# Two graph attention layers: the edge bytes are turned by VectorE in 32x32 blocks, masked on ScalarE, in groups of eight row tiles

## The reference

```python
def _L0_gnn_ref(input, W, a, adj, M):        # input: h, 8192 x 128; M = 8192
    h = input @ W
    e = jax.nn.leaky_relu((h[:M] @ a[:OUT, 0])[:, None] + (h @ a[OUT:, 0])[None, :], negative_slope=ALPHA)
    valid = (adj[:M] > 0) & (h.sum(axis=1) != 0)[None, :]
    att = jnp.where(valid, jax.nn.softmax(jnp.where(valid, e, NEG), axis=1), 0.0)
    L = valid.sum(axis=1).astype(h.dtype)
    top = att.max(axis=1)
    attention = jnp.where(att >= THR, att, 0.0) * L[:, None]
    attention = jnp.where((top > THR)[:, None], attention, 0.0)
    return jax.nn.elu(h[:M] + attention @ h)

def _L1_gnn_ref(h, adj, W, a):
    Wh = h @ W
    e = jax.nn.leaky_relu((Wh @ a[:F_out, 0])[:, None] + (Wh @ a[F_out:, 0])[None, :], negative_slope=ALPHA)
    return jax.nn.softmax(jnp.where(adj > 0, e, NEG_INF), axis=1) @ Wh

h = jnp.maximum(_layernorm(x, axis=-1), 0.0)     # x: 8192 x 128 f32, adj: 8192 x 8192 int32
x = x + _L0_gnn_ref(h, L0_gnn_W, L0_gnn_a, adj, 8192)
h = jnp.maximum(_layernorm(x, axis=-1), 0.0)
x = x + _L1_gnn_ref(h, adj, L1_gnn_W, L1_gnn_a)
```

## Time and profile before

| | us |
|---|---|
| median of 3 runs (2136.21 to 2138.7) | 2136.89 |
| the profiled execution, its own time | 2139.07 |
| its span, first to last instruction | 2137.3 |
| TensorE busy | 2010.9 (94%) |
| VectorE busy | 1561.5 (73%) |
| ScalarE busy | 806.9 (38%) |
| GpSimd busy | 638.6 (30%) |

### The profile page before, as it was taken

One profiled execution on the slowest core, in us unless ns is written; L12 is line 12 of the kernel. 1 busy time (PEld: TensorE's weight loads), 2 busy tenths in 40 slices (PEclk: granted clock), 3 DMA queues, 4 the chain that ended last, 5 costly groups with the idle time before them and its releaser, 6 DMA issues. The chain is left out here.

```text
span 2137.3 us, 43514 instructions
## 1 busy us (share of the span) xinstructions
PE 2010.9 (94%) x17812; PEld 2003.4 (94%) x17812; DVE 1561.5 (73%) x2452; ACT 806.9 (38%) x950; POOL 638.6 (30%) x263
## 2 busy tenths in 40 slices
PE   5699999999999999999965699999999999999997
PEld 4699999999999999999965699999999999999997
DVE  6687777777777777777747677777777777777775
ACT  4677777777777777777734000000000000000000
POOL 0675655575655575656510000000000000000000
PEclk9899999999999999999987799999999999999998
DMA  7889888899888899888832522323222323222230
GB/s 227 331 341 375 318 329 318 334 373 362 334 316 327 323 384 359 323 328 327 331 130 79 190 69 70 99 80 100 80 81 60 98 79 99 80 73 79 68 99 11
DMA packets 112206, 447.75 MB, mean 209 GB/s; under 512 B 8320, under 2 KB 57984, under 8 KB 62592
## 3 DMA queue, kind: packets, MB, share of 16 engines
q1 hardware_dynamic: 112000, 444.89, 56.4%
HBM read 365.04 MB, written 79.82 MB: 208 GB/s over the span
## 5 line engine op out<-in xcount | busy, mean ns | idle before, releaser
L984 PE MATMUL psum<-h_all,arena 128*128 128x129 f32 x8192 | 960.0, 275 | 0.2 <-DVE arena L1007 0.2
L1163 PE MATMUL psum<-h_all,arena 128*128 128x129 f32 x8192 | 919.4, 275 | 24.7 <-DVE arena L1180 24.7
L1163 PEld LDWEIGHTS psum<-h_all,arena 128*128 128x128 f32 x8192 | 917.9, 192 | 26.4 <-issue 17.3
L984 PEld LDWEIGHTS psum<-h_all,arena 128*128 128x128 f32 x8192 | 937.5, 192 | 1.2 <-issue 0.5
L1007 DVE SCALAR_TENSOR_TENSOR arena<-arena,rho_col,psum 128x512 f32<-128x512 uint8 (+1 forms) x1024 | 693.8, 742 | 235.6 <-PE psum L970 218.3
L1180 DVE SCALAR_TENSOR_TENSOR arena<-arena,rho_col 128x1024 f32<-128x1024 f32 (+1 forms) x512 | 653.3, 1284 | 235.4 <-PE psum L1163 222.9
L911 POOL TENSOR_SCALAR arena<-arena 128x2048 uint8<-128x2048 int32 x256 | 637.6, 2526 | 441.8 <-DMA arena<-in_adj_dram 293.4
L929 ACT ACTIVATE arena<-arena 128x2048 bf16<-128x2048 uint8 x256 | 487.8, 1906 | 35.1 <-POOL arena L911 35.1
L940 ACT ACTIVATE arena<-psum 128x1024 uint16<-128x1024 uint16 x256 | 261.1, 1020 | 251.0 <-DVE arena L1007 250.4
L970 PE MATMUL psum<-ident,arena 128*128 128x128 f32 x1024 | 154.4, 274 | 14.5 <-POOL arena L911 14.5
L970 PEld LDWEIGHTS psum<-ident,arena 128*128 128x128 f32 x1024 | 121.1, 142 | 14.7 <-POOL arena L911 14.7
(11 more groups left out here) (100 smaller groups left out, 191.8 us busy)
## 6 DMA issues: line engine op xcount, KB each, us to landing
arena<-in_adj_dram SPq DMA_DIRECT2D x256, 1024.0 KB, 9.8
edgesT<-arena SPq DMA_DIRECT2D x64, 1024.0 KB, 7.6
arena<-edgesT SPq DMA_DIRECT2D x64, 1024.0 KB, 8.8
arena<-r_mid SPq DMA_DIRECT2D x2, 3072.0 KB, 13.8
h_mid<-h_all SPq DMA_DIRECT2D x16, 256.0 KB, 2.3
arena<-in_x_dram SPq DMA_DIRECT2D x16, 256.0 KB, 3.1
arena<-h_mid SPq DMA_DIRECT2D x16, 256.0 KB, 3.9
x_mid<-arena SPq DMA_DIRECT2D x16, 256.0 KB, 2.4
```

What stands on the lines that cost most here:

```text
L984: last = nc.tensor.matmul(acc_tile(g, G0, k), wTs[m % WRING][:, k * P:(k + 1) * P], h_all[:, j, :], start=(j == 0 and k % 2 == 0), stop=(j ...
L1163: last = nc.tensor.matmul(acc_tile(g, G1, k), wTs[m % RING][:, k * P:(k + 1) * P], h_all[:, j, :], start=(j == 0 and k % 2 == 0), stop=(j ...
```

## The change

**Layout.** The partitions of a piece are no longer 128 rows of one row tile. A row tile is now 32 rows out of each quarter of the matrix (row `a*2048 + t*32 + i` with a in 0..3), and a piece of adjacency has, on its 128 partitions, four blocks of columns by 32 rows, 1024 columns each (0.5 MB, in 4 KB rows). With the words laid out so, turning every 32 x 32 block in place of the 128 x 128 one gives the same bytes at the place where a form wants them. x, h and the outputs are read or written by quarters of 32 partitions where they must follow.

**Masks.** ScalarE writes the bytes itself, as sigmoid(200 a - 100), straight out of the int32 piece, and counts with the same instruction's accumulator (`mask_piece`). GpSimd has no part in layer 0 any more. The counts are then in four parts on the wrong partitions: VectorE adds the halves and four small products on TensorE with a constant matrix `rows_of` bring them together (`join_counts`).

**Turns.** VectorE turns 1024 words per instruction (`turn_edges`), eight instructions for each *chunk* (eight row tiles by half of the columns, 32 pieces), two halves of four row tiles each; they go between the forms at fixed tiles (`turn_at`). The result lies in SBUF in five slots `edges` and is stored to `edgesT` from there; TensorE's transposes and the copies out of PSUM go.

**Groups.** Layer 0 works in 8 groups of eight row tiles, as layer 1, with the same form and product instructions, and its finish is cut in five steps between forms (`finish_at`). All 8 PSUM banks hold sums.

**Preparation.** The 32 pieces of chunk 0 are loaded, masked and turned within the preparation of layer 0, and six pieces more are loaded. Sigmoid, square root and exponential are in different ACT tables, so tables are loaded between them. **Layer 1** reads whole blocks of 1 MB in 8 KB rows, in a ring of five, the first one ahead of r_row; its finish reads the eight denominators in one instruction each, and its outputs are stored by quarters.

The four stores of a chunk stand among its first pieces. The diff, cut:

```diff
+G = 8
+GW = G * P
+NG = T // G
+BK = 4
+HALVES = 2
+COLS = 2
+LC = N // BK // COLS
+CT = T // COLS
+SBT = 8
+SUBS = CT // SBT
+NSUB = T // SBT
+PIECES = HALVES * BK * BK
+NA = 6
+ER = 5
+RING = 4
+FOLDS = 8
 CB = CH // P
...
+        edgesT = nc.dram_tensor("edgesT", [NG * NSUB, P, SBT * GW], U8, kind="Internal").ap()
...
+        adj_in = [part(4 * N - (NA - i) * LC, LC).bitcast(I32) for i in range(NA)]
...
+        adj_pieces = adj.rearrange("(a t i) (b c n) -> t a c b i n", a=BK, i=BP, b=BK, c=COLS)
...
+        def piece(n):
+            g, r = n // (COLS * PIECES), n % (COLS * PIECES)
+            c, r = r // PIECES, r % PIECES
+            h, k, a = r // (BK * BK), r // BK % BK, r % BK
+            return g, c, h, k, a
+        def load_piece(sp, n):
+            g, c, h, k, a = piece(n)
+            if n >= NA:
+                sp.wait_ge(masked, n - NA + 1)
+            sp.dma_start(adj_in[n % NA], adj_pieces[g * G + 2 * k + h, a, c])\
+                .then_inc(adj_in_loaded[n % NA], 16)
+        def mask_piece(act, n):
+            g, c, h, k, a = piece(n)
+            act.wait_ge(adj_in_loaded[n % NA], 16 * (n // NA + 1))
+            if n >= PIECES and k == 0 and a == 0:
+                act.wait_ge(turned, turn_number(n // PIECES - 1, h, SUBS - 1))
+            nc.scalar.activation(pack_bytes[h][:, k, a], adj_in[n % NA].rearrange("p (m j) -> p m j", j=BP),
+                                 ACT.Sigmoid, bias=half_step[:, 0:1], scale=STEEP,
+                                 accum_out=cnt[g % 2][:, a, 2 * k + h, c:c + 1]).then_inc(masked, 1)
+        def turn_number(chunk, h, s):
+            return chunk * HALVES * SUBS + h * SUBS + s + 1
+        def turn_edges(dve, chunk, h, s):
+            block = chunk * SUBS + s
+            if s == 0:
+                dve.wait_ge(masked, chunk * PIECES + (h + 1) * BK * BK)
+            if block >= ER and h == 0:
+                dve.wait_ge(edges_stored[block % ER], 16 * (block // ER))
+            nc.vector.transpose(edge_words[:, block % ER, h],
+                                packs[h][:, s * SBT * P:(s + 1) * SBT * P].rearrange("p (b i) -> p b i", b=SBT))\
+                .then_inc(turned, 1)
...
+                    nc.gpsimd.memset(rows_of[:], 0.0).then_inc(made, 1)
+                    pool.wait_ge(made, 3)
+                    for a in range(BK):
+                        for b in range(BK):
+                            q = slice(b * BP, (b + 1) * BP)
+                            nc.gpsimd.tensor_copy(rows_of[q, a, a * BP:(a + 1) * BP], ident[q, q])
...
-            x_all = weights[0].rearrange("p (t f) -> p t f", f=F)
-            hn = weights[1].rearrange("p (t f) -> p t f", f=F)
+            x_all = part(N, N).rearrange("p (t f) -> p t f", f=F)
+            hn = x_all
...
+                        if first:
+                            for b, rows in each_quarter():
+                                sp.dma_start(x_all[rows, c, :], rows_in(x_in)[b, :, c, :]).then_inc(x_loaded[i], 16)
+                            load_piece(sp, i)
+                        else:
+                            sp.dma_start(x_all[:, c, :], x_view[:, c, :]).then_inc(x_loaded[i], 16)
                     if first:
-                        for k in range(G0):
-                            sp.dma_start(adj_in[k], adj_view[2 * k, :, 0, :]).then_inc(adj_in_loaded[k], 16)
+                        for m in range(XP, 2 * NA):
+                            load_piece(sp, m)
                         for q in range(Q):
                             wait(sp, h_kept, 2 * Q, 2 * (q + 1))
                             sp.dma_start(h_view[:, q * QT:(q + 1) * QT, :], h_all[:, q * QT:(q + 1) * QT, 0:F])\
                                 .then_inc(h_stored, 16)
+                            for m in range(2 * NA + 2 * q, min(2 * NA + 2 * q + 2, PIECES + NA)):
+                                load_piece(sp, m)
...
                             normalise(q)
+                    if first:
+                        for h in range(HALVES):
+                            for s in range(SUBS):
+                                turn_edges(dve, 0, h, s)
...
+                    if first:
+                        for m in range(NA):
+                            mask_piece(act, m)
                     deviation(0)
                     for q in range(Q):
                         if q % (Q // XP) == 0 and q // (Q // XP) < XP - 1:
...
                         nc.scalar.activation(hnT[q % 2], hn_ps[q % 2], ACT.Relu, accum_out=hn_sums[:, q:q + 1])\
                             .then_inc(hnT_ready, 1)
+                        if first:
+                            for m in range(NA + 2 * q, min(NA + 2 * q + 2, PIECES)):
+                                mask_piece(act, m)
                         if q >= 1:
...
+                def store_block(block):
+                    sp.wait_ge(turned, turn_number(block // SUBS, HALVES - 1, block % SUBS))
+                    sp.dma_start(edgesT[block], edge_blocks[:, block % ER]).then_inc(edges_stored[block % ER], 16)
+                def store_out(g):
+                    sp.wait_ge(out_ready, g + 1)
+                    sp.dma_start(out_view[g], tiles(ye)).then_inc(stored, 16)
+                def load_residuals(g):
+                    if g >= 1:
+                        sp.wait_ge(acc_read, g)
+                    sp.dma_start(tiles(hr), h_view[g]).then_inc(hr_loaded, 16)
+                    if g >= 1:
+                        sp.wait_ge(out_ready, g)
+                    for b, rows in each_quarter():
+                        sp.dma_start(tiles(xr)[rows], x_view[b, :, g * G:(g + 1) * G, :]).then_inc(xr_loaded, 16)
+                load_r(sp, r_loaded, 0)
+                for chunk in range(1, NG * COLS + 1):
+                    for i in range(PIECES):
+                        ahead = chunk * PIECES + i + NA
+                        if ahead < NG * COLS * PIECES:
+                            load_piece(sp, ahead)
+                        if i in (4, 7, 10, 13):
+                            store_block((chunk - 1) * SUBS + (i - 4) // 3)
+                        if chunk == 1 and i == 14:
                             load_r(sp, r_loaded, 1)
                             load_r(sp, r_loaded, 2)
+                        if chunk % COLS == 0:
+                            g = chunk // COLS - 1
+                            if i == 2 and g >= 1:
+                                store_out(g - 1)
+                            if i == 16:
+                                load_residuals(g)
+                store_out(NG - 1)
...
+                def elu(g):
+                    act.wait_ge(acc_read, g + 1)
+                    nc.scalar.activation(ye, yy, ACT.Relu, scale=-1.0).then_inc(y_neg_ready, 1)
+                    act.wait_ge(y_neg_ready, g + 1)
+                    nc.scalar.activation(ye, ye, ACT.Exp, scale=-1.0).then_inc(y_exp_ready, 1)
+                for chunk in range(1, NG * COLS):
+                    for i in range(PIECES):
+                        mask_piece(act, chunk * PIECES + i)
+                        if chunk % COLS == 1 and chunk > 1 and i == 26:
+                            elu(chunk // COLS - 1)
+                elu(NG - 1)
...
+                    elif step == 3:
+                        dve.wait_ge(y_exp_ready, g + 1)
+                        link(nc.vector.scalar_tensor_tensor(ye, ye, -1.0, yy, ALU.add, ALU.max))
...
+                finish_at = {5: 0, 7: 1, 9: 2, 14: 3, 16: 4}
+                turn_at = {15: (0, 0), 17: (0, 1), 19: (0, 2), 24: (0, 3), 25: (1, 0), 27: (1, 1), 29: (1, 2), 31: (1, 3)}
...
                     for j in range(T):
+                        m = g * T + j
+                        if j % SBT == 0:
+                            dve.wait_ge(turned, turn_number(m // CT, HALVES - 1, j // SBT % SUBS))
+                        if m >= RING:
+                            dve.wait_ge(summed, m - RING + 1)
+                        form_tile(g, j, wTs[m % RING]).then_inc(formed, 1)
                         if g == 0 and j % (T // FOLDS) == 0 and j < T - T // FOLDS:
                             fold(h_folded, j // (T // FOLDS) + 1)
+                        if g >= 1 and j in finish_at:
+                            finish(g - 1, finish_at[j])
+                        if m // CT + 1 < NG * COLS and j % CT in turn_at:
+                            h, s = turn_at[j % CT]
+                            block = (m // CT + 1) * SUBS + s
+                            if block >= ER:
+                                dve.wait_ge(formed, (block - ER + 1) * SBT)
+                            turn_edges(dve, m // CT + 1, h, s)
+                        if j == 36:
+                            nc.vector.tensor_reduce(quarter_counts[:], cnt[g % 2][:], AX.X, ALU.add)\
+                                .then_inc(quartered, 1)
...
+                def load_block(block):
+                    if block >= ER:
+                        sp.wait_ge(formed, (block - ER + 1) * SBT)
```

(2 more changed lines are left out.)

537 lines of the change are left out of this document (201 added, 336 removed).

## The result

The changed kernel takes **3922.9 us** (median of 3 runs, 3921.64 to 3925.12), the kernel before 2136.89: ratio 1.8356, 95% interval 1.8315 to 1.8398. The forecast was 2094. Its profiled span is 3923.3 us. From the page: DMA queue 1, then groups of instructions (line, count, busy us, mean ns, idle before and who ended it).

The account below looks back on a forecast made before the run. TensorE sets the pace of both layers, transposes paid in full: preparation +35.0, layer 0 -67.7, joints +3.6, -8.3 and -5.6 give -43.0 from the median 2136.89, forecast 2094 us, range 2062 to 2150.

Parts of the forecast that it names:

- the price of the 4 KB piece: Layer 0's adjacency loads: 160 ns per 4 KB packet on each of 16 engines, 410 GB/s, 1.28 us per 0.52 MB piece.
- Rival (c): 4 KB pieces load at a lower rate; at 300 GB/s a group needs 137 us, total 2235; chance 0.07.
- pieces under 334 GB/s: Sign of being wrong: layer 0's adjacency pieces load below 334 GB/s, the rate from which rival (c) decides.
- The turns: VectorE in layer 0: a turn of 1024 words takes 1.2 us, 16 turns per group 19 us.
- Bare layer 0: Layer 0 without stalls, TensorE's products setting the pace: 926.9 us.
- The elu's wait: VectorE waits 5 us per group for the elu's Exp in layer 0; TensorE loses 3.6, six groups 21.6.
- The mask: ScalarE's masking of one adjacency piece: 1.15 us with issue, priced by the 1024-wide copy plus accumulator read.
- rival (d): Masks dearer: at 1.9 us ScalarE needs 61 us for a chunk of 57.3; total about 2190; chance 0.06.
- The preparation: Work before layer 0's sums gets longer: first sum at 109.6 instead of 74.6, 35.0 us more.
- estimate of 4.8 us for the quarter loads: Layer 0's x loads of 32 partitions, reaching 8 of 16 ports, take some 4.8 us longer; total 2099.
- Group 0: Layer 0's first group: chunk 1's loads take 52 us where VectorE wants it at 46, costing 4.0 us.
- Joints: Layer 0's end +3.6 us, layer 1's first sum 8.3 earlier, seven group ends in layer 1 -0.8 each.

Follow-up runs that it names:

- the rows outermost: Changed kernel with adjacency loads' DRAM pattern [32, 4, 1024] in place of [4, 32, 1024], values landing on other partitions: 2229.3 us, ratio 1.0447.
- the mask cheaper and the wait moved: Changed kernel with row index outermost in its loads, Identity for the mask's Sigmoid, and elu steps after forms 22 and 23: 2121.0 us, ratio 0.9935.

## Why the prediction was wrong, step by step

**The step that failed** is "each of 16 engines" in the price of the 4 KB piece: four engines did the work, and a piece took 4.99 us and not 1.28. The price per packet was right: 160 ns forecast, 4.99 us for 32 packets on each of 4 engines measured, 156 ns. The number of engines was assumed, from rows of loads whose outermost dimension is 128. The forecast looked at the length of a row and not at the dimensions around it, though the diff shows both patterns. Rival (c) stood at the right place with the wrong lower end: it took x's 294 GB/s for the worst case, and the 105 was outside the range that any row of loads could bound. Of the prediction's own signs of being wrong, pieces under 334 GB/s is the one that came.

The rule was to be had. The Trainium skill, "DMA: Bandwidth & Descriptors", Why a DMA increments its semaphore by 16 and not by 1, has the largest k up to 16 that divides the slowest dimension of both sides, and one completion write for each engine used. The runs agree: each load leaves 2, 4, 8 or 16 short packets as its outermost dimension is 2, 4, 8 or a multiple of 16. An estimate by that rule has a piece at four times 1.28, 5.1 us, and the 474 pieces behind the first 38 alone at 2400 us.

In the 1829 us between forecast and result, layer 0 has 1693 (2654.8 for 961.8) and the preparation 136.6 (246.2 for 109.6): there 38 pieces stand before the joint, and SyncE's stores of h, d and r in one queue with them.

With the rows outermost, the other steps can be read:

- **The turns**: right. A turn is 1237 ns (1.2 forecast).
- **Bare layer 0**: close. With the mask cheaper and the wait moved, TensorE's products take 939 us at a mean granted clock of 0.98, where the forecast has 926.9, and its stops 32. That the sum, 971, lies near the forecast's 961.8 is luck: its 34.9 of stalls were mostly the elu's, and here the elu's step is moved.
- **The elu's wait**: this is the larger part of what was left with 16 engines. The place was right, the size was not. Forecast: VectorE at +20.9, Exp ready at +25.9, TensorE loses 3.6. Measured in the group whose first form is at 401.37: VectorE stops at 424.1 (+22.7), the Exp ends at 441.1 (+39.7), TensorE stands 13.8; over layer 0 the seven such stops are 102 of the 127.6 us. The first of the 27 masks starts at -11.9, not at -17.3, because the masks before it were late; the 27 masks take 48.2 us, not 39.8. Of these 37.8 are masks at 1.385 to 1.40 each and 10.4 waits for pieces. The Relu and the Exp behind the last mask:

```profile
437.67 1.04 ACT L975 ACTIVATE arena<-arena 128x1024 f32<-128x1024 f32 x1
...
440.02 1.06 ACT L977 ACTIVATE arena<-arena 128x1024 f32<-128x1024 f32 x1
```

  The pieces came late because the DMA engines were full, not for a delay of the single load. The window over the 27 masks, with the share 1.00 and 381 GB/s:

```profile
389.40:437.70 48.30, 39.30 (x350) 38.92 (x348) 32.84 (x38) 37.90 (x57) 0.00 (x0) 0.97 1.00 381
```

  27 loads and four stores pass in it, 18.3 MB. The forecast let 21 loads and the four stores pass at 410 GB/s, with six pieces already in the ring when the masks began.

- **The mask**: 1.15 forecast, 1.385 from one to the next. This is a third of the way to rival (d) (1.9), and the wait above takes it 27 times.
- **The clock**: a term that the forecast had at nothing. It is 19 of the 112 us with the rows outermost, by the sum above.
- **The preparation**: +35.0 forecast, +56.9 with all engines. The first inverse is at 45.2 us instead of 33.7: quarter loads of x at 205 to 236 GB/s (7 us of it by the run with whole loads), the six masks, and constants that delay SyncE's first load by 4.2 us, where I had put in 2.3. The prediction's estimate of 4.8 us for the quarter loads does not follow from the two rates that it gives, and 7 was measured. The 26 masks behind it add 6 us by their price, and 5.1 are waits for pieces.
- **Group 0**: TensorE stands 15.7 us once, 4.0 forecast.
- **Joints**: right. Last sum to store 8.9 us (9.0 forecast); last sum of layer 0 to first of layer 1 87.1 us for 92.1, -5.0 (forecast +3.6 - 8.3); a group of layer 1 114.84 us for 115.83, seven times -1.0 (forecast -0.8).

Even with 16 engines the sign would have been wrong: +22 and +112 turn -43 into +91, and 92 was measured. The sum compared averages of a group, 107 us of DMA and 102 of VectorE in 115.6, which leaves 9 and 14 of room. In front of the elu there was none, and there the late masks, their price and the full DMA engines added up.

## What to carry to other kernels

For every load, write down the dimensions on the DRAM side and look at the outermost before its bytes: it, not the row length, decided here how many engines work, and a DMA share that stays at 4/16 while an engine waits for DMA is the sign of it. Next ask how many partitions one load covers. When a wait is moved, follow what the moved step releases: here a store, and behind it in the same queue the loads that everything waits for.

## What the hardware showed that I had not expected

- The number of engines follows the outermost dimension: 105 GB/s at 4, half of it at 2 (52 at share 0.13), 4.9 to 5.1 us per MB at 8; 26 GB/s for each engine in all three.
- Loads into 32 or 64 partitions occupy all 16 engines, with a share of 1.0 and more, and move 205 to 262 GB/s, where one of 128 reaches 409. The profile shows a full DMA in both cases.
- An outermost dimension of 16 with groups of 8 rows gave only 254 to 288 GB/s in most windows, near or far apart. Not explained.
- The software queue kept the 4 KB rows whole, added 400 packets under 512 B to each load, and moved 144 to 230 GB/s with all engines occupied.
- TensorE ran at a granted clock of 0.50 in a stop of 15 us, and at a mean of 0.73 in the 10 us behind it: 63 records for 92.
- ScalarE needs 1429 ns for 1024 int32 into every fourth byte, and 1365 with Identity, for 1020 of a copy.
